# Four transformer stages in one kernel: layers written out, and three pieces of weight conversion moved

## The reference

```python
ada = silu(c) @ W_ada + b_ada
shift_msa, scale_msa, gate_msa, shift_mlp, scale_mlp, gate_mlp = split(ada, 6)
h = modulate(layernorm(x), shift_msa, scale_msa)
x = x + gate_msa * attention(h)        # 16 heads of 18, softmax, projection
h = modulate(layernorm(x), shift_mlp, scale_mlp)
x = x + gate_mlp * (gelu(h @ W_fc1 + b_fc1) @ W_fc2 + b_fc2)
```

## Time and profile before

| | us |
|---|---|
| median of 3 runs | 2093.96 |
| lowest and highest run | 2091.3, 2096.46 |
| the profiled execution's own time | 2095.36 |
| its span in the profile | 2093.7 |
| mean granted clock of TensorE | 0.967 |
| half steps begin at about | 201 |

### The profile page before, as it was taken

The page is one execution under the profiler, slowest core; times in us unless marked ns, Lnnn a source line. Parts: engine busy times, 40 slices in busy tenths (PEclk is TensorE's granted clock), DMA queues, the critical chain, the costliest instruction groups (busy, mean ns, idle before and its releaser), DMA issues. The chain is left out here.

```text
span 2093.7 us, 49820 instructions
## 1 busy us (share of the span) xinstructions
PE 1977.5 (94%) x16599; PEld 1757.2 (84%) x16599; DVE 1205.1 (58%) x2656; ACT 1120.6 (54%) x1928; POOL 1006.7 (48%) x1037
## 2 busy tenths in 40 slices
PE   5886799999999999899999999998999999999996
PEld 3554589899999998789899998997889998999986
DVE  7874556556465575556565465575565465554641
ACT  5322464655656645555655646555555646556552
POOL 1002455455554554655454454555655554555534
PEclk9787899999999999999999999999999999999998
DMA  7514433333323333433333323333433323333320
GB/s 204 134 61 120 145 101 80 103 90 92 99 80 106 97 84 102 152 100 90 94 87 101 99 80 103 91 92 99 135 86 99 99 79 105 92 91 96 84 81 26
DMA packets 138467, 207.01 MB, mean 99 GB/s; under 512 B 35720, under 2 KB 95718, under 8 KB 137318
## 3 DMA queue, kind: packets, MB, share of 16 engines
q1 hardware_dynamic: 110338, 168.31, 29.2%
q10 hardware_dynamic: 25332, 29.74, 5.2%
q0 software_dynamic: 2704, 7.77, 1.4%
HBM read 99.18 MB, written 20.82 MB: 57 GB/s over the span
## 5 line engine op out<-in xcount | busy, mean ns | idle before, releaser
L2255 DVE TENSOR_REDUCE maxima<-scores 128x4 f32<-128x1024 f32 x384 | 460.9, 1223 | 180.4 <-PE scores L2011 173.4
L1618 POOL TENSOR_TENSOR hidden<-g_full,hidden 128x512 fp32r<-128x512 f32 (+1 forms) x240 | 280.5, 1176 | 356.6 <-ACT hidden L1852 355.4
L1809 ACT ACTIVATE probs<-scores 128x1024 f32<-128x1024 f32 x384 | 383.2, 1027 | 98.7 <-PE pv_ps L2048 58.8
L2073 PE MATMUL mlp_ps<-h_mlp,w_up 128*128 128x256 f32 (+1 forms) x3024 | 404.6, 286 | 5.0 <-POOL h_mlp L1618 3.4
L2073 PEld LDWEIGHTS mlp_ps<-h_mlp,w_up 128*128 128x128 f32 (+1 forms) x3024 | 378.6, 190 | 35.4 <-issue 19.4
L1936 PE MATMUL mlp_ps<-w_down,hidden 128*128 128x288 f32 x2592 | 390.8, 296 | 0.0
L1936 PEld LDWEIGHTS mlp_ps<-w_down,hidden 128*128 128x128 f32 x2592 | 370.0, 189 | 18.6
L2011 PE MATMUL scores<-k_stack,q_stack 108*128 108x512 f32 x768 | 241.9, 407 | 8.9 <-DMA k_stack<-qk 6.8
L2034 PE MATMUL scores<-q_stack,k_stack 110*128 110x256 f32 x1536 | 247.0, 293 | 3.4 <-ACT probs L1809 2.2
L2034 PEld LDWEIGHTS scores<-q_stack,k_stack 110*128 110x128 f32 x1536 | 209.3, 192 | 33.0 <-issue 18.9
L1799 ACT ACTIVATE neg_max<-att_ps 16x256 fp32r<-16x256 f32 x48 | 17.9, 374 | 380.9 <-PE att_ps L2021 380.9
(11 more groups left out here) (263 smaller groups left out, 2843.4 us busy)
## 6 DMA issues: line engine op xcount, KB each, us to landing
q_stack<-qk SPq DMA_DIRECT2D x144, 180.0 KB
k_stack<-qk SPq DMA_DIRECT2D x282, 90.0 KB
inv_sum<-inv_scratch ACTq DMA_DIRECT2D x192, 128.0 KB, 2.7
k_stack<-qk SPq DMA_DIRECT2D x282, 54.0 KB
x_mid<-out_x SPq DMA_DIRECT2D x48, 288.0 KB, 4.2
out_x<-x_out SPq DMA_DIRECT2D x48, 288.0 KB, 3.1
x_in<-out_x SPq DMA_DIRECT2D x46, 288.0 KB, 3.9
q_stack<-qk SPq DMA_DIRECT2D x144, 72.0 KB
```

What stands on the lines that cost most here:

```text
L1618: tt(out, full, high.bitcast(F32), ALU.subtract).then_inc(signal, 1)
L1809: evict(probs[:, u % 4, :, :, :], scores[u % 2][:, :, :, :], ACT.Exp, scale=SCALE)\
L2073: last = mm(up_bank[n % 2][:, (m % 2) * T:(m % 2 + 1) * T], w[:, m * P:(m + 1) * P], h, start=count == 0, stop=count == 6)
L2255: nc.vector.tensor_reduce(out=maxima[:, :, :, u], in_=scores[u % 2][:, :, :, :], axis=AX.X, op=ALU.max).then_inc(s_max, 1)
```

## The change

**Layers written out.** `whole_run` loops over the three layers in Python, so each layer's code stands in the program with a constant l; the loops over b stay.

**Value columns.** In half step (l,15) VectorE's conversion of the "v" columns of the next layer moves from behind the norm and normalisation of sample it+2 to directly behind `mlp_high`.

**w_up.** ScalarE makes all high parts of w_up at the end of half step (l,0), and none at the start of (l,1). The low parts of the two large pieces go from GpSimd to VectorE (`low_up`): the first at the end of (l,0), the second in (l,1) between `gate_projection` and `mlp_norm`. GpSimd keeps the three small ones in (l,1), now all behind the inverse deviation with a wait for it, and issues the DMAs of the pieces that follow in the staging slots later, behind the deviation of sample it+2 (`stage_followers`). SyncE loads layer 0's pieces 9 and 10 in its prologue. The counts that the engines wait for are changed to fit.

```diff
--- before.py
+++ after.py
@@ -1461,38 +1461,37 @@
-        BY_VECTOR = [*((n, "down") for n in OF["w_down"]), *((n, "down") for n in OF["b_down"]),
+        BY_VECTOR = [*((n, "up") for n in OF["w_up_raw"]), *((n, "down") for n in OF["w_down"]), *((n, "down") for n in OF["b_down"]),
                      *((n, "qk") for n in OF["w_in"]), *((n, "v") for n in OF["w_in"])]
-        BY_OTHERS = [*OF["w_out"], *OF["w_up_raw"], *OF["w_up"]]
+        BY_SCALAR = [*OF["w_out"], *OF["w_up_raw"], *OF["w_up"]]
+        BY_POOL = [*OF["w_out"], *OF["w_up"]]
         def converted(n, l):
-            return len(BY_OTHERS) * l + BY_OTHERS.index(n) + 1
+            return len(BY_SCALAR) * l + BY_SCALAR.index(n) + 1
+        def converted_by_pool(n, l):
+            return len(BY_POOL) * l + BY_POOL.index(n) + 1
...
             ahead = 2 * len(OF["w_in"])
-            if part == "down":
+            if part in ("up", "down"):
                 return len(BY_VECTOR) * l + ahead + BY_VECTOR.index((n, part)) + 1
...
             half_step(0, 0)
-            with engine.Fori(0, L - 1) as l:
+            for l in range(L):
                 half_step(l, 1)
...
                 half_step(l, B - 1)
-                half_step(l + 1, 0)
-            half_step(L - 1, 1)
-            with engine.Fori(2, B - 2) as b:
-                half_step(L - 1, b)
-            half_step(L - 1, B - 2)
-            half_step(L - 1, B - 1)
+                if l < L - 1:
+                    half_step(l + 1, 0)
             epilogue()
...
@@ -1568,6 +1567,7 @@
             def prologue():
+                raw_weights("w_up", up_raw[:, :, :], 0, s_up, PRE, 0)
                 negated_maxima(0)
...
@@ -1582,7 +1582,7 @@
                     stacks(it + 1)
-                if at(b, 0):
+                if at(b, 0) and before:
                     raw_weights("w_up", up_raw[:, :, :], l, s_up, UP_USES * it + PRE, 0)
...
@@ -1617,22 +1617,23 @@
-            def low_weights(name, l, which=None, last_layer=False):
-                for n in OF[name] if which is None else [OF[name][k] for k in which]:
-                    p = pieces[n]
-                    rows = p["low_rows"]
+            def low_weights(name, l):
+                for n in OF[name]:
                     pool.wait_ge(s_w_high, converted(n, l))
-                    for high, low_part, full in conversion(n, rows):
+                    if name == "w_up":
+                        pool.wait_ge(s_w_low, converted_by_pool(n, l) - 1)
+                    for high, low_part, full in conversion(n, pieces[n]["low_rows"]):
                         last = tt(low_part, full, high.bitcast(F32), ALU.subtract)
                     last.then_inc(s_w_low, 1)
-                    follower = (l, n + SLOTS) if n + SLOTS < NP else (l + 1, n % SLOTS)
-                    pool.wait_ge(s_w_low, converted(n, l))
-                    if n >= NP:
-                        continue
-                    if n + SLOTS < NP or not last_layer:
-                        stage(pool, *follower)
+            def stage_followers(name, l, last_layer=False):
+                for n in OF[name]:
+                    pool.wait_ge(s_w_low, converted_by_pool(n, l))
+                    if n + SLOTS < NP:
+                        stage(pool, l, n + SLOTS)
+                    elif not last_layer:
+                        stage(pool, l + 1, n % SLOTS)
...
@@ -1657,6 +1658,7 @@
                 low_weights("w_out", 0)
+                stage_followers("w_out", 0)
...
@@ -1666,14 +1668,18 @@
                 if at(b, 1):
-                    low_weights("w_up_raw", l, (1,))
-                    low_weights("w_up", l, last_layer=last_layer)
+                    pool.wait_ge(s_rstd[1], it)
+                    low_weights("w_up", l)
+                    pool.wait_ge(s_w_low, converted_by_pool(OF["w_up"][-1], l))
                 if before:
...
                     inverse_deviation(0, it + 2)
+                if at(b, 1):
+                    stage_followers("w_up", l, last_layer)
                 if at(b, 0) and before:
                     low_weights("w_out", l)
+                    stage_followers("w_out", l)
                 if before:
...
@@ -1693,8 +1699,6 @@
                     add_mlp(it - 1, 1)
-                if at(b, 0):
-                    low_weights("w_up_raw", l, (0,))
...
@@ -1861,9 +1865,6 @@
                 negate_maxima(it)
-                if at(b, 1):
-                    high_weights("w_up_raw", l, (1,))
-                    high_weights("w_up", l)
                 for n in range(3):
...
@@ -1907,7 +1908,8 @@
                 if at(b, 0):
-                    high_weights("w_up_raw", l, (0,))
+                    high_weights("w_up_raw", l)
+                    high_weights("w_up", l)
...
@@ -2091,7 +2093,7 @@
                 if part is None:
-                    pe.wait_ge(s_w_low, converted(n, l))
+                    pe.wait_ge(s_w_low, converted_by_pool(n, l))
                 else:
...
@@ -2134,6 +2136,7 @@
                         weights_ready("w_up", l)
+                        weights_ready("w_up_raw", l, "up")
                     up(m, 0)
...
@@ -2247,6 +2250,14 @@
+            def low_up(l, k):
+                n = OF["w_up_raw"][k]
+                dve.wait_ge(s_w_high, converted(n, l))
+                dve.sem_inc(s_v_high, 1)
+                for high, low_part, full in conversion(n, pieces[n]["low_rows"]):
+                    tt(low_part, full, high.bitcast(F32), ALU.subtract).then_inc(s_v_low, 1)
...
@@ -2311,6 +2322,8 @@
                     gate_projection(it - 1)
+                    if at(b, 1):
+                        low_up(l, 1)
                     mlp_norm(it - 1)
...
@@ -2324,6 +2337,10 @@
                     mlp_high(it - 1)
+                if at(b, B - 1) and after:
+                    dve.wait_ge(s_v_ps, 2 * it + 2 + PRE)
+                    convert_weights(l + 1, OF["w_in"], "v")
                 if after_next:
...
@@ -2337,10 +2354,6 @@
                     convert_weights(l + 1, OF["w_in"], "qk")
-                if at(b, B - 1) and after:
-                    dve.wait_ge(s_v_ps, 2 * it + 2 + PRE)
-                    convert_weights(l + 1, OF["w_in"], "v")
                 inverse(it)
...
@@ -2353,6 +2366,8 @@
                     gate_down(it - 1, 1)
+                if at(b, 0):
+                    low_up(l, 0)
```

## The result

The changed kernel takes 2079.11 us in the median of 6 runs (2073.99 to 2082.45), the kernel before beside it 2094.41 (6 runs, 2091.3 to 2098.02): ratio 0.9931, 95% interval 0.9913 to 0.9948. By the ratio that is 14.4 us less, between 10.9 and 18.2; the two medians are 15.3 apart. Run again later on another chip it took 2081.78 (6 runs) beside 2094.18, ratio 0.9951 (0.9933 to 0.9969); all 12 runs together have a median of 2081.4. The forecast was 2083.5, range 2070 to 2090.5, faster.

The account below looks back on a forecast made before the run. TensorE, busy 94% of the 2093.7 us span, was taken as the bound. Terms -5.65 - 1.9 - 4.8 + 1.6 = -10.75 us gave 2084.6 from the profiled execution, 2083.2 from the median; written 2083.5, range 2070 to 2090.5.

Parts of the forecast that it names:

- The jump: End of half step (1,0): writing the layers out removes the jump back of the layer loop, gaining 5.65 us.
- The constants: 24 inner steps of layers 0 and 1: the layer as a constant saves 0.08 us each, 1.9 in all.
- The value columns: Step 15 at two layer ends: earlier conversion cuts TensorE's idle from 4.87 to 2.45 us, gaining 4.8 in all.
- w_up: Step 1 of each layer: the moved w_up work changes when the MLP's transposes start, costing 1.6 us in all.
- Case (a): Step 1 of each layer: GpSimd's small w_up pieces do not shut VectorE out; time 2070, chance 0.15.
- (b): Each step 1 and each layer end: VectorE becomes the bound, 6.1 us worse, 2089.5; chance 0.12.
- (c): Layers' first steps: stalls of new code replace the jump's; one leaves 2089, four make 2106; chance 0.05 for three or four.
- (d): At the layer loop's jump: written-out code does not gain but keeps one such stop, 2089; chance 0.06.

Follow-up runs that it names:

- e1: The kernel before with the loop over layers written out and nothing else; 2083.71 us, ratio 0.9953.
- e12: e11 with w_up's two loads in half steps (1,0) and (2,0) issued behind the second hidden low part; 2058.98 us, ratio 0.9837.
- e8: The changed kernel itself, run again unaltered on another chip; 2081.78 us, ratio 0.9951.
- e7: The changed kernel with the value columns of w_in converted where they were before the change; 2087.51 us, ratio 0.9973.
- e2: e1 plus the value columns converted behind the MLP's high part, w_up as in the kernel before; 2075.6 us, ratio 0.992.
- e10: The changed kernel with w_in's two large loads issued in half step (l,2) instead of (l,1); 2070.62 us, ratio 0.9884.
- e9: e5 with w_in's two large loads issued in half step (l,2), behind the deviation of the MLP norm; 2060.69 us, ratio 0.9857.
- e4: The changed kernel with GpSimd's small w_up pieces behind VectorE's normalisations instead of behind the deviation; 2072.61 us, ratio 0.9914.
- e11: e9 with the value columns' casts in (l,15) behind the MLP's normalisation and their subtractions ahead of the MLP's high part; 2059.23 us, ratio 0.9835.
- e3: The changed kernel with w_in's two loads behind the hidden low parts instead of ahead of them; 2080.76 us, ratio 0.9936.
- e5: e4 with w_in's two loads at the very end of GpSimd's part of half step (l,1); 2065.5 us, ratio 0.9874.
- e6: e5 with VectorE's subtraction of w_up's second large piece moved behind the MLP's high part; 2070.36 us, ratio 0.9904.

## Why the prediction was right, point by point

**The jump, -5.65.** Measured -4.54 in step (1,0), and nothing at "issue" is left. With the outer jump back gone, the stall is gone (e1). That edit takes away the jump and the register of the layer together, so that it was the jump is argued, from the place of the stop. The term was too large by 1.1, because I took (2,0)'s 38.30 as what the same work costs without a jump. Written out, GpSimd issues w_up's loads earlier, ahead of the store of the sums, and both (1,0) and (2,0) get a stop at the third up product. For (2,0) that is +1.85, a term that my sum lacks. That these loads delay the store is shown by e12, where the store is on time once they are moved. The Trainium skill, "Runtime: NRT & Kernel Launch", section "Instruction fetch mechanics", says that a taken branch whose target lies outside the fetched pages stalls. The trace agrees for the outer jump, with 2.30 and 1.84 us at "issue" before and none after; no run separates the fetch from other causes. The inner jumps show no stop in steps of 37.8 us, before or after.

**The constants, -1.9.** Measured on the eleven inner steps of layers 0 and 1: 37.855 to 37.783 and 37.860 to 37.746, together -2.0. Right; e1 has it by itself.

**The value columns, -4.8.** Measured -3.5 and -6.1 in (0,15) and (1,15), -9.7 together, and -8.2 in e8; undone alone, 7.2 by the sums (e7), done alone, 7.4 in these two steps (e2 against e1). The order was as I wrote, as far as the trace shows it: the casts end behind GpSimd's subtraction. Two sizes were off. The stop is 1.85 and not 2.45, because GpSimd's subtraction ends 0.5 us earlier against TensorE's due time than in the trace of before (1402.87, due 1402.90; before 1415.43, due 1414.99), and from there to the end of the conversion it is 1.82. And the shorter stop left the clock at 1.00 in three of the changed kernel's four such steps, so that the slow matmuls behind it went too. I had named that and left it out of the sum. It was worth about 2 a layer (e10: 41.83 against 39.84; by the difference of steps and stops, 0.5 in (0,15) and 3.1 in (1,15)).

**w_up, +1.6.** Measured +2.2, +3.3 and -4.2 in (0,1), (1,1), (2,1): +1.3. The sum comes out and its parts do not, and it is no firmer than the single executions it is taken from: the three steps (l,1) took 135.1 in the kernel before, but 131.5 in e1 and 134.4 in e2 with the same code for w_up. I had +0.1, +2.6 and -1.1. The normalisations at 3.4 (3.75 forecast) and the transposes at T + 10.4, 10.7 and 10.95 (10.7, 11.4, 11.4) are as worked out, a little better. But the step that counted the DMAs of the moved code is missing: I costed the staging loads, which moved with GpSimd's work, at nothing and named no transfer beside them. The late store of the sums costs 2 to 5 us in each of (0,1) and (1,1) (e10: 43.59 and 42.48 instead of 47.28 and 46.44, or 45.80 and 46.15 in e8; e9 against e4: 3.9 and 5.3). What covered that error is the earlier transposes, the clock in (2,1), and the luck of the execution before: its (2,1) took 46.88, where e1 and e2 took 44.02 and 45.24 behind the same stop of 3.60. The page "SBUF — State Buffer" of the Trainium skill, section "Who interferes with whom", says that a VectorE instruction with two SBUF inputs contends with a GpSimd instruction that reads SBUF, which spoke against this part. The trace agrees: GpSimd's two attention adds take 2.69 beside VectorE's subtraction instead of 0.8 each. It was in my order of work. What I took as given is that GpSimd's small pieces run beside the normalisations: e4, which puts them behind, is worth 10.8 by the sums.

**The rivals.** Case (a), small pieces that let the normalisations through, did not come: 3.4 us, not 1.3. Its time, 2070, is what e4 and e10 reach by other edits. (b) did not come: the transposes are not beyond T + 12. (c) and (d) did not come: no idle at "issue" at a layer's first steps.

**The sum.** -4.5 + 1.85 - 2.0 - 9.7 + 1.3 = -13.1, and +1.2 in the other steps, mostly (2,14), where the row of negated maxima came late (39.55; in e8 38.20, so this is the execution's): -11.9 against -10.75. The forecast from the median before, 2083.2, stands beside 2079.1 of the first runs and 2081.4 of all 12. Part of the closeness is luck: an error of -4.9 at the values and one of +1.85 plus some 1 at the jump went against each other, and in w_up the unseen late store was offset as said.

The best kernel, e12 or e11, takes 2059, a ratio of 0.984 to before. It differs from the changed kernel in where GpSimd subtracts and loads and in the order of VectorE's conversion, and in no work.

## What to carry to other kernels

When GpSimd work moves, list each DMA that moves with it, and beside its new place each small transfer that an engine waits for at once; a load of some hundred KB ahead of such a transfer cost TensorE 1 to 4 us here, and moving the load by one queue position only helps if the next small transfer isn't met instead (e3, e5 and e12 each met the next one, e9 found the gap). Put a GpSimd subtraction behind a VectorE operation that sets the end, not beside it: one changed wait (e4) brought 10.8 us by the sums, 6.5 to 8.8 by the medians. And where two profiled executions are compared, cut them at a mark and compare piece by piece, since a stage that nobody changed can differ by 5.6 us between two runs of one program.

## What the runs showed of the hardware that I had not expected

- A 16 KB store to DRAM and the wait for it take 1.9 us from its issue to the issue of the read in an ordinary step, 2.5 with one 147 KB load issued ahead of it and one 0.6 behind, 3.0 to 4.1 with both ahead, and 4.5 to 5.9 with two loads of 432 KB issued 3 to 5 us ahead (changed kernel, e4). Such loads are not the only cause: in (0,1) of e12, with none of them ahead, it took 3.1.
- Behind the same stop of 1.84 to 1.88 us ahead of the same product, TensorE's granted clock was 1.00 in some executions and steps and 0.57 to 0.67 in others, and the step 2 us longer. Behind the changed kernel's stops of 2.6 to 2.8 us ahead of the transposes the clock was low (in (2,1) 0.68 over the 3.2 us from 1481.80 on); behind e9's stop of 0.66 at the same place it stayed at 1.00.
- GpSimd's five hidden low parts took 9.68 us together beside VectorE's conversions of w_down and b_down (e6), where an ordinary step has the five done in 6.8 us, 1.3 for one alone.
